# Results of the expert stage split into two kinds of passes, second weights kept, next attention's preparation between the rounds

## What is computed

```python
# layer 2, g = 32 tokens of a group, 16 groups in each of 8 batches, 128 experts
grouped = x.reshape(b, s // g, g, d)
logits = jnp.einsum('bntd,des->bntes', grouped, Wc) + bc
perm = (logits == jnp.max(logits, axis=-3, keepdims=True)).astype(x.dtype)
permuted = jnp.einsum('bntd,bntes->bnesd', grouped, perm)
inner = jax.nn.relu(jnp.einsum('bnesd,esdf->bnesf', permuted, W1) + b1)
result_permuted = jnp.einsum('bnesf,esdf->bnesd', inner, W2) + b2
result = jnp.einsum('bnesd,bntes->bntd', result_permuted, perm)
# layer 3 starts with x + tanh(g_ffn[0]) * result, its norm, and q = norm @ Wq.T + bq
```

## Time and profile before

| | us |
|---|---|
| median of 3 runs | 1487.01 |
| lowest, highest | 1486.59, 1489.23 |
| profiled execution | 1493.08 |
| its span in the profile | 1491.2 |
| its mean granted PE clock | 0.934 |

### The profile page before, as it was taken

How to read it: one execution, slowest core, us unless ns; L and a number is a source line. 1 busy time by engine, 2 the same in 40 slices (tenths; PEclk the granted TensorE clock), 3 DMA queues, 4 the chain that set the end, 5 groups by cost and what they waited for, 6 DMA issues and landing times.

```text
span 1491.2 us, 27798 instructions
## 1 busy us (share of the span) xinstructions
PE 1317.2 (88%) x10496; PEld 952.4 (64%) x10496; DVE 901.6 (60%) x1596; ACT 575.3 (39%) x1037; POOL 373.5 (25%) x324
## 2 busy tenths in 40 slices
PE   6977999999999879766579999999996889999997
PEld 5755677777777667511156667657664667777776
DVE  5885466665676446544356566565754477777772
ACT  4452444335433455433124323432341443333331
POOL 2541110111011100040033113311321654444441
PEclk9998999999999989965579999999998899999999
DMA  9995243134412575799755425533512301111111
GB/s 336 308 310 169 77 141 108 70 124 139 139 50 83 185 213 161 262 422 403 309 201 169 158 69 167 196 121 103 167 48 85 114 29 56 56 56 56 56 38 48
DMA packets 129235, 223.69 MB, mean 150 GB/s; under 512 B 24598, under 2 KB 45590, under 8 KB 125070
## 3 DMA queue, kind: packets, MB, share of 16 engines
q1 hardware_dynamic: 129166, 222.73, 43.6%
HBM read 131.47 MB, written 91.23 MB: 149 GB/s over the span
## 4 chain that ended last, share of the span: by engine, by line
PE 42%; issue 26%; DVE 12%; ACT 8%; POOL 7%; DMA 4%; SPq 1%; POOLq 0%; DVEq 0%; ACTq 0%
PE b L145 5%; PE b L146 5%; PE b L147 5%; PE b L1849 4%; PE b L1414 3%; PE b L1566 3%; PE b L1567 2%; PE b L1568 2%; PE b L1817 2%; DVE f_mix L2012 2%; PE b L1485 2%; PE b L1494 2%; ACT e_gt L1758 2%; POOL f_xmrl L1974 2%; PE b L1387 2%
## 5 line engine op out<-in xcount | busy, mean ns | idle before, releaser
L1070 ACT ACTIVATE a_pr<-b 120x512 f32<-120x512 f32 x256 | 133.8, 601 | 94.3 <-PE b L1414 94.3
L1211 DVE TENSOR_REDUCE a_mx<-b 128x4 f32<-128x480 f32 x256 | 151.2, 651 | 3.6 <-PE b L1387 3.6
L1000 POOL TENSOR_TENSOR a_atl<-a_pvs,a_ath 128x512 fp32r<-128x512 f32 x64 | 81.4, 1295 | 228.3 <-ACT a_ath L1113 228.3
L962 POOL TENSOR_TENSOR a_rstd<-a_ve,a_mhalf 128x4 f32<-128x4 f32 x16 | 16.2, 1012 | 443.2 <-DVE a_ve L1160 443.2
L1566 PE MATMUL b<-a_woh,a_ath 128*128 128x512 f32 x256 | 105.9, 414 | 3.6 <-POOL a_atl L1000 3.6
L145 PE MATMUL b<-a_xth,a_wqh 128*128 128x512 f32 x256 | 104.2, 407 | 1.5 <-issue 1.5
L1567 PE MATMUL b<-a_wol,a_ath 128*128 128x512 f32 x256 | 102.9, 402 | 0.0
L1568 PE MATMUL b<-a_woh,a_atl 128*128 128x512 f32 x256 | 102.3, 400 | 0.0
L146 PE MATMUL b<-a_xtl,a_wqh 128*128 128x512 f32 x256 | 102.2, 399 | 0.0
L147 PE MATMUL b<-a_xth,a_wql 128*128 128x512 f32 x256 | 102.0, 399 | 0.0
L1309 DVE SCALAR_TENSOR_TENSOR a_x<-b,a_gate,a_x 128x512 f32 (+1 forms) x64 | 47.8, 747 | 86.3 <-PE b L1568 86.3
(11 more groups left out here) (215 smaller groups left out, 3205.8 us busy)
## 6 DMA issues: line engine op xcount, KB each, us to landing
s_rp<-e_gt SPq DMA_DIRECT2D x32, 1024.0 KB, 8.6
a_rp<-s_rp SPq DMA_DIRECT2D x32, 1024.0 KB, 9.9
s_x<-a_x SPq DMA_DIRECT2D x16, 1024.0 KB, 4.3
kv_xb<-in_x SPq DMA_DIRECT2D x8, 1024.0 KB, 7.8
s_xn<-kv_xb SPq DMA_DIRECT2D x8, 1024.0 KB, 9.7
a_xn<-s_xn SPq DMA_DIRECT2D x8, 1024.0 KB, 7.6
a_x<-in_x SPq DMA_DIRECT2D x8, 1024.0 KB, 6.0
s_xn<-a_xn SPq DMA_DIRECT2D x8, 1024.0 KB, 5.0
```

Source lines behind the costliest of these rows:

```text
L1070: act.activation(pr[:, h % RING, :], bank[k][0:S2, :], ACT.Exp, scale=SCALE)\
L1211: dve.tensor_reduce(mx[:, t, :, r], bank[k][:, 0:HJ * S2].rearrange("p (a s) -> p a s", a=HJ), AX.X, ALU.max).then_inc(free[k], 1)
```

## The change

**Two kinds of passes.** The 128 groups are now in the order of the batches. The results of batches 0 and 1 (32 groups, `FIRST`) are computed in passes of their own, `first_groups(j)`: four products of 32 x 32 by 512, one on each quarter of rows and of columns, all into one bank, evicted as a whole. Four of them follow each of the rounds 6 to 13 (`LEAD_AT`, `LEADS`, `lead_after`), in banks 4 and 5 in turns. The 32 rounds of `results(k)` now take 96 groups, in banks 0 to 3 alone, into a ring of four rounds. Each store of a round has 96 partitions (768 KB); the lead passes are stored four at a time as four transfers of 32 partitions (256 KB each) from two buffers.

**All second weights kept.** The four parts of the second weight have places of their own; the third and fourth (2048 KB each) are issued ahead of the first store.

**The preparation between the rounds.** Loads, ACT's, DVE's and PE's work for batch 0 of the second attention are placed behind rounds 7 to 31 (`behind` in each engine, `load_behind` on SP). The maxima before the first turn use two banks (`MT`), the transposed norm the banks `t` and `w`. From round 22 on ACT evicts three banks of a round and DVE one (`REST_SPLIT`). The load of the output weight and its split move into the first turn.

Core of the diff:

```diff
+LEAD_AT, LEADS, REST_SPLIT = 6, 4, 22
...
+            k, uses = MT[t % 2]
+            return k, uses.n(None, "max", 2 * r + t // 2)
+        return f"s{t}", S.n(i, "max", r)
...
-        if k is None:
-            sp.wait_ge(cleared, 1)
-            load_query_weight(sp)
+        if k == 7:
+            sp.wait_ge(front.cleared, 1)
             load_x(sp, 0)
+            load_perm(sp, 0)
+            sp.dma_start(b2[:, :], io["b2"]).then_inc(w_in[2], 16)
             load_gates(sp)
             sp.dma_start(bq[:, :], io["bq"]).then_inc(c_in, 16)
-        if k == 10:
-            load_perm(sp, 0)
-            sp.dma_start(b2[:, :], io["b2"]).then_inc(w_in[2], 16)
-
-    def weights_act(act, k):
-
-        if k == 20:
-            act.wait_ge(cleared, 1)
-            act.wait_ge(w_in[2], 16)
-            act.activation(b2h[:, :], b2[:, :], ACT.Copy).then_inc(e_hi, 1)
-            act.wait_ge(c_in, 16 * 3)
-            act.activation(gate[:, :], gate[:, :], ACT.Tanh).then_inc(gated, 1)
-            query_weights_high(act)
...
+            front.written(sp, 0)
+            load_x(sp, 1)
             for k, uses in TW:
                 sp.wait_ge(full[k], uses.n(None, "merge", 1) + 1)
             load_perm(sp, 1)
             for t in range(NT):
                 load_experts(sp, 1, t)
-            load_x(sp, 1)
+            for q in range(1, 4):
+                front.written(sp, q)
+            load_output_weight(sp)
...
+            if k == 11:
+                act.wait_ge(front.cleared, 1)
+                act.wait_ge(w_in[2], 16)
+                act.activation(b2h[:, :], b2[:, :], ACT.Copy).then_inc(e_hi, 1)
+                act.wait_ge(c_in, 16 * 3)
+                act.activation(gate[:, :], gate[:, :], ACT.Tanh).then_inc(gated, 1)
+            if k == 12:
+                query_weights_high(act)
+            if k == 21:
+                first_norm(None, range(C))
+            if k in (23, 24):
+                queries(None, (k - 23,))
+            if k in (26, 28):
+                queries(None, (k // 2 - 11,))
+            if k == EK - 1:
+                negated_max(None)
...
+                steps = Steps(dve, dchain, 2)
+                for t in range(NT):
+                    ins = merged(steps, None, 0, t)
+                variance(steps, 0, ins)
+            if k == 20:
+                apply(xs[:, 0], 0)
+            if k == 21:
+                first_norm(None, 0, range(C))
+            if k in (23, 24):
+                queries(0, (k - 23,))
+            if k in (25, 27, 29, 30):
+                maxima(None, {25: 0, 27: 1, 29: 2, 30: 3}[k])
+            if k in (26, 28):
+                queries(0, (k // 2 - 11,))
+            if k == EK - 1:
+                dve.wait_ge(bo_in, 16)
+                dve.tensor_scalar(bo[:, :], bo[:, :], gate[:, 0:1], None, ALU.mult).then_inc(bo_gated, 1)
...
+                pe.wait_ge(front.cleared, 1)
+                pe.wait_ge(e_lo, 1)
+                front.spare_banks(pe)
+                for t in range(NT):
+                    merge_tile(None, 0, t)
+            if k == 21:
+                first_norm(None, range(C))
+            if k == 23:
+                pe.wait_ge(w_lo[0], C)
+            if k in (23, 24):
+                queries(None, k - 23)
+            if k in (25, 27, 29, 30):
+                if k == 25:
+                    pe.wait_ge(const, 4)
+                    pe.wait_ge(kbd_in, 16 * HJ)
+                for t in range(NT):
+                    max_tile(None, 0, {25: 0, 27: 1, 29: 2, 30: 3}[k], t)
+            if k in (26, 28):
+                queries(None, k // 2 - 11)
+            if k == EK - 1:
+                max_rows(None)
+                front.banks(pe)
+                scores(None, 0, 0)
...
-    RB, RO, KS, RW = 6, 6, 8, 4
+    RB, RO, KS, RW = 6, 4, 8, 4
+    FIRST = 2 * GB
...
+    flat = gt[0][:, :, :].rearrange("p e n -> p (e n)")
+    out = flat[:, 2 * KB:10 * KB].rearrange("p (q e d) -> p q e d", q=RO, e=EJ)
+    lead = [flat[:, 10 * KB:12 * KB].rearrange("p (q d) -> p q d", d=D), w1[:, :, :, :].rearrange("p r e f -> p r (e f)")]
+    by_step = lambda a: a.rearrange("p (k d) -> p k d", d=D)
+    w2 = [by_step(x[:, :, :].rearrange("p n d -> p (n d)")) for x in (*xc, chosen)] + [by_step(flat[:, 12 * KB:16 * KB])]
...
+    def rest_on_act(k, a):
+
+        return a < 2 or (a == 2 and k >= REST_SPLIT)
+
+    def lead_bank(j):
+
+        return 4 + j % 2, uses(4 + j % 2, SETS * C) + j // 2
+
+    def lead_after(k):
+
+        return range(LEADS * (k - LEAD_AT), LEADS * (k - LEAD_AT + 1)) if 0 <= k - LEAD_AT < EK // LEADS else ()
...
-        behind[0].load(sp, None)
+                    load_w2(sp, 0, s)
         for s in range(WG - RW):
+            load_w2(sp, 1, s)
             sp.wait_ge(h_full[s % 2], (SETS * (C - 1) + s) // 2 + 1)
             load_w1(sp, WG * (C - 1) + s + RW)
-        load_w2(sp, 1)
+        load_w2(sp, 2, 0)
+        load_w2(sp, 3, 0)
         for k in range(EK):
             for a in range(EJ):
-                b, n = use(first_result(k), a)
-                sp.wait_ge(g_free[b], n + 1)
-            sp.dma_start(io["rp"][:, EJ * k:EJ * (k + 1), :], out[:, k % RO]).then_inc(out_st[k % RO], 16)
+                sp.wait_ge(g_free[a], uses(a, SETS * C) + k + 1)
+            sp.dma_start(io["rp"][FIRST:, EJ * k:EJ * (k + 1), :], out[0:NG - FIRST, k % RO]).then_inc(out_st[k % RO], 16)
+            if lead_after(k):
+                store_lead(sp, k - LEAD_AT)
             behind[0].load(sp, k)
-            if k % KS == KS - 1 and k // KS + 2 < EK // KS:
-                load_w2(sp, k // KS + 2)
-        for q in range(RO):
-            sp.wait_ge(out_st[q], 16 * len(range(q, EK, RO)))
+
+    def store_lead(sp, h):
+
+        for j in range(LEADS * h, LEADS * (h + 1)):
+            b, n = lead_bank(j)
+            sp.wait_ge(g_free[b], n + 1)
+        of = io["rp"][0:FIRST].rearrange("n (h k a) d -> h a n k d", a=EJ, k=LEADS)[h]
+        for a in range(EJ):
+            sp.dma_start(of[a], lead[h % 2][a * FIRST:(a + 1) * FIRST]).then_inc(lead_st[h % 2], 16)
+
+    def lead_written(sp):
+        for h in range(2):
+            sp.wait_ge(lead_st[h], 16 * EJ * (EK // LEADS // 2))
+
+    def written(sp, q):
+        sp.wait_ge(out_st[q], 16 * len(range(q, EK, RO)))
...
+                    act.wait_ge(g_full[a], uses(a, SETS * C) + k + 1)
+                    act.activation(out[0:NG - FIRST, k % RO, a], gbank[a][0:NG - FIRST, :], ACT.Copy)\
+                       .then_inc(g_free[a], 1)
+            for j in lead_after(k)[0::2]:
+                h = j // LEADS
+                if h >= 2 and j % LEADS < 2:
+                    act.wait_ge(lead_st[h % 2], 16 * EJ * (h // 2))
+                b, n = lead_bank(j)
                 act.wait_ge(g_full[b], n + 1)
-                act.activation(out[:, k % RO, a], gbank[b][:, :], ACT.Copy).then_inc(g_free[b], 1)
-            behind[0].weights_act(act, k)
+                act.activation(lead[h % 2][:, j % LEADS], gbank[b][:, :], ACT.Copy).then_inc(g_free[b], 1)
+            behind[0].act(act, k)
...
+                pe.matmul(gbank[a][0:NG - FIRST, :], inner[rows, k, FIRST:], w2[k // KS][rows, k % KS, :], start=True,
+                          stop=True).then_inc(g_full[a], 1)
+            for j in lead_after(k):
+                first_groups(j)
+            behind[0].pe(pe, k)
+
+        def first_groups(j):
+
+            if j == 0:
+                pe.wait_ge(relued, WG)
+            if j % KS == 0:
+                pe.wait_ge(w2_in[j // KS], 16 * QUARTERS[j // KS])
+            b, n = lead_bank(j)
+            pe.wait_ge(g_free[b], n)
+            for a in range(EJ):
+                rows = slice(a * EF, (a + 1) * EF)
+                ins = pe.matmul(gbank[b][a * FIRST:(a + 1) * FIRST, :], inner[rows, j, 0:FIRST],
+                                w2[j // KS][rows, j % KS, :], start=True, stop=True, skip_group_check=True)
+            ins.then_inc(g_full[b], 1)
...
```

More of the change, by code:

```diff
@@ L823, in weights_dve @@
[L823 to L835 removed]
+        if k == 9:
+            load_query_weight(sp)
@@ L997, in turn @@
                 after[0].mixes_low(pool, 0, 0)
+            if merge and first_turn(i):
+                low_parts(pool, 1)
             for g in range(C):
@@ L1101, in turn @@
                 second_norm(i, (2, 3))
+            if merge and first_turn(i):
+                output_weights_high(act)
             if merge and not last:
@@ L1556, in turn @@
                     max_tile(i, i + 1, 1, t)
+            if merge and first_turn(i):
+                pe.wait_ge(w_lo[1], C)
             if merge and last_:
@@ L1776, in results @@
                 dve.wait_ge(out_st[k % RO], 16 * (k // RO))
-            for a in (2, 3):
-                b, n = use(first_result(k), a)
+            for a in range(EJ):
+                if not rest_on_act(k, a):
+                    dve.wait_ge(g_full[a], uses(a, SETS * C) + k + 1)
```

(10 more changed lines are left out.)

258 lines of the change are left out of this document (125 added, 133 removed).

## The result

| | before | after |
|---|---|---|
| median of 4 runs each | 1487.69 us | 1509.84 us |
| lowest, highest | 1486.59, 1489.23 | 1507.85, 1511.24 |
| ratio, 95% interval | | 1.0147, 1.013 to 1.0165 |
| span of the profiled execution | 1491.2 | 1509.5 |

The account below looks back on a forecast made before the run. It saw rounds half waiting for evictions, saturated transfers nobody waits for, an 8.17 us PE gap, then the preparation. Terms put Z at 787.5 against 791.28 (-3.8); 8 for small waits made +4: 1491 us, range 1478 to 1508.

Parts of the forecast that it names:

- Start of the stores: Before round 6: evictions of the fifth round wait for the first store, queued behind 7.3 MB of loads; +2.7 us.
- Rounds 6 to 13: The rounds with lead passes: five passes each, transfers 42 us and PE 43, taken as 45 us; +19.
- rival D: Lead passes stay at the lower clock or do not run together: 10 us a round, +35, 1526; chance 0.07.
- Rival B: Narrow stores last by partitions, not bytes: eight lead rounds 67 us instead of 45, +16, 1507; chance 0.23.
- Rounds 14 to T0: Last rounds with the preparation between them, from round 14 at 688 to the first scores at 765; 77 us.
- T0: Start of the first scores, 778.28 us in the kernel before; predicted at 765.
- The gain of 13 us at T0: First scores 13 us earlier: the 8.2 us gap gone, the last 13 rounds sharing time with the preparation.
- The wait after T0: After the first scores, PE waits about 9 us for batch 1's late-issued `a_rp` before its first merge; +8.
- Z: End of the fourth merge of batch 1, 791.28 us before; predicted at 786, before Output weight and small waits.
- Output weight: In turn 0, ACT's four weight copies stand ahead of its first transposed-norm copy; +1.5 us, bounds 0 and 2.2.
- The 8 us for small waits: Added over the whole stretch, because the same sum for the kernel before put Z at 783; +8 us.
- Rival C: Missing 8 us were the old kernel's own, denser PE keeps the higher clock through rounds 14 to 31; 1479, chance 0.25.

Follow-up runs that it names:

- e7: Changed kernel with the two 2048 KB second-weight loads issued behind the stores of rounds 3 and 7 instead of ahead of the first store; 1507.6 us.
- e1: Changed kernel with all stores of results, rounds' and lead passes', leaving from 128 partitions, same bytes, output no result of the task; 1498.5 us.
- e9: Changed kernel with lead results in DRAM by expert, then group, four lead passes stored as one 1024 KB transfer from 128 partitions; 1510.4 us.
- e12: Changed kernel with one wide lead store, early a_rp of batch 1, and 2.5 MB of second-attention loads behind rounds 13 and 16; 1511.6 us.
- e6: Changed kernel with all lead passes and evictions, but only 2 of each lead transfer's 32 partitions stored, output no result of the task; 1499.9 us.
- e5: Changed kernel with lead passes stored one by one from 128 partitions, 256 KB each, to a destination of 4 x 32 rows; 1567.0 us.
- e8: Changed kernel combining the parts of e5, e3 and e7: one-by-one lead stores, early a_rp of batch 1, late weight loads; 1553.5 us.
- e16: Changed kernel with wide lead store by expert, early a_rp of batch 1, late weight loads, and 2.3 MB of loads out of the lead rounds; 1495.2 us.
- e3: Changed kernel with batch 1's permutation and a_rp loads issued behind rounds 22 to 28 instead of behind the last store; 1501.0 us.
- e13: Changed kernel with the 96 groups' results alternating between partitions 0 to 95 and 32 to 127 from round to round; 1512.2 us.
- e4: Kernel before with each 1024 KB store made as two, from 96 and 32 partitions; 1513.4 us, ratio 1.0167.
- e10: Changed kernel with lead results by expert as in e9, but each lead pass stored by itself, 256 KB from 128 partitions; 1505.3 us.
- e18: Kernel before with each 1024 KB store made as two of 128 partitions x 2 banks; 1491.7 us, ratio 1.0000.

## Why the prediction was wrong

*Start of the stores* (+2.7, round 6 at 643.3). The mechanism was right: round 5 waits 11.36 us for the first store. Too small by 3.3: rounds 0 to 6 took 27.9, the prediction's own numbers say 24.7. The first store was issued at 625.72 and landed 17.6 us later, at 643.3, not at 638.8. The prediction let the loads run at 387 GB/s from 616.5 on; from 616.5 to 621.5 it was 229, in the 5 us after that 321. Round 0 itself was 1.9 later, ahead of all that the sum covers; it lies between 615.4 and 622.9 in the runs of changed kernels. e7 shows that the two large loads are the whole wait.

*Rounds 6 to 13* (45 us predicted, 59.8 measured). This is the step that failed. A lead pass was sized rightly (four in 3.86 us, 0.97 each; 4.84 a round at the higher clock, 4.85 predicted), and rival D is out: the granted clock was 0.85 in the window from 646 to 700. What failed is "0.79 + 1.05 MB a round is 4.4 us at 420 GB/s": that rate was measured on 128-partition stores. The rounds' transfers then need longer than PE's five passes, by the rate of 271 GB/s at a share of 0.92: 55 us of full engines, where the prediction had 42. Wide stores give back 11.1 of the 14.8 us (e1). Loads out of the way give back 9.6 with wide lead stores (e9 to e12), the lead stores' bytes 11.6 (e6); these shares overlap, since all of them shorten one full queue, and no run has both wide stores and the loads away. So what the other 3.7 are stays open. Rival B named this mechanism and gave 1507, with a chance of 0.23; I took the rate that the trace showed against a rule for which it had no row, and weighed "no row" as if it spoke against.

*Rounds 14 to T0* (77 us predicted). 78.5, and 77.8 to 79.2 in all other changed kernels but e5 and e8 (88.8 and 87.1), e12 (98.4) and e16 (83.4), where stores or loads come late. Wide stores (e1, 78.7) and 4.2 MB more of loads (e3, 78.5) do not change it, so there it is not the transfers that set it.

*The gain of 13 us at T0* did not come: T0 was 786.65, 8.4 later than before, since all losses lie ahead of it.

*The wait after T0* (+8). PE idle 8.86 us, the end of the list of loads as told; T0 to Z is 23.2 instead of 21, and e3 shows that the wait is the queue's order. It was named `a_rp`; the first to be waited for was the permutation, one place ahead in the queue.

*Output weight* (+1.5). The first scores of batch 1 come at

```profile
849.66 0.50 PE L1451 MATMUL b<-a_qh,a_kbd 32*120 32x512 f32 x4
```

39.85 us after Z, and before

```profile
829.93 0.50 PE L1414 MATMUL b<-a_qh,a_kbd 32*120 32x512 f32 x4
```

it was 829.93 - 791.28 = 38.65. So 1.2, from one execution each.

*The 8 us for small waits.* Misses in the terms add up to 1.9 + 3.3 + 14.8 + 1.5 + 2.2 = 23.7 us; the 8 took up a third. Z came 16 later than the prediction's, which is also what rival B adds. That its 1507 lies so near is in part luck: the lead rounds were 14.8 later, the other terms 8.9, and the 8 happened to meet them.

*Rival C* had round 14 on, with a denser PE, 5 us faster. Not so.

## What to carry to other kernels

Before a store is split or narrowed to free work earlier, price it by its partitions, not by its bytes, and above all when the queue is full anyway: here the narrow stores cost 11 us, and 23 in the kernel before. In a full queue a load moved away from one wait turned up in the next (e7, e16); what helped was faster or fewer bytes, or a place where the queue has room (batch 1's operand among the last rounds: 9 us for a change of order alone). Test what an enabling step costs by itself: the split passes and their stores took 24 us for a placement worth 6 to 16.

## What the runs showed of the hardware that I had not expected

- A 768 KB store from 96 partitions landed in 4.3 us at the least, from 128 partitions in 3.2. In the kernel before, 1024 KB stored as 96 + 32 partitions brought the rate from 418 to 327 GB/s at a busy share of 0.96 instead of 1.01; as 2 x 128 partitions it was 412 at 1.03.
- Narrow transfers in a row that complement each other in partitions were no faster than alike ones (e13: 1512.2 us, the changed kernel 1509.8; e4 was 23 us slower than whole stores).
- A destination of 4 x 32 rows, 256 KB from group to group, instead of 128 rows next to each other took the rate from 301 to 179 GB/s, and the busy share from 0.89 to 0.56 (e10, e5).
- An issue on SP can take long: 0.33 us for a round's store in the kernel before (median, at a transfer share of 1.01), 1.3 us for each of the 32-partition stores in the changed one (median), and all that stands behind them on SP waits. Two issues for one in the kernel before (e18, 0.43 us each) cost nothing that can be told. What makes SP stand was not tested.
- Four quarter products of 32 x 32 x 512 run together at 0.97 us, like the four quarter products of 120 x 32.
